# Where the last sweep's bounds, sums and weighted results are made in a one-core graph and expert layer

## The reference

```
x1   = x + segment_sum((ln(x) @ Wg)[src] * w[:, None], dst) + b_g
xf   = ln(x1)
top_w, top_i = top_k(xf @ Wgate + bgate, 2);  top_w = softmax(top_w)
out  = x1 + sum over the two chosen experts e of
           top_w[e] * (gelu(xf @ W1[e] + b1[e]) @ W2[e] + b2[e])
```

## Time and profile before

| what | value |
|---|---|
| median of 3 runs | 900.51 us (893.99, 900.51, 902.76) |
| the profiled execution | 891.33 us, its span 889.6 us |
| mean granted clock of TensorE | 0.942 of full speed |
| PE busy | 716.7 us, 81% |
| DVE busy | 486.4 us, 55% |
| ACT busy | 347.0 us, 39% |
| POOL busy | 605.5 us, 68% |
| q0 (GpSimd's indirect transfers) | 69.14 MB |
| q1 (SyncE's transfers) | 67.56 MB |
| q10 (ScalarE's transfers) | 50.97 MB |

### The profile page before, as it was taken

The page is one execution under the profiler, slowest core; times in us unless marked ns, Lnnn a source line. Parts: engine busy times, 40 slices in busy tenths (PEclk is TensorE's granted clock), DMA queues, the critical chain, the costliest instruction groups (busy, mean ns, idle before and its releaser), DMA issues. The chain is left out here.

```text
span 889.6 us, 15451 instructions
## 1 busy us (share of the span) xinstructions
PE 716.7 (81%) x5265; PEld 703.1 (79%) x5265; DVE 486.4 (55%) x1333; ACT 347.0 (39%) x629; POOL 605.5 (68%) x607
## 2 busy tenths in 40 slices
PE   1067669787199998988899999999999876898891
PEld 0067668686199998978899999989998876898890
DVE  5514212344235477584247867844556877667760
ACT  4312000101024455344244653635546552567770
POOL 6377777777677777777777787777788737023553
PEclk9999999997589999798899999999999999899996
DMA  7897864796468888793888799677767964647742
GB/s 202 260 356 214 226 198 116 203 276 188 123 189 254 246 248 255 203 284 109 230 246 291 227 278 306 192 200 233 254 206 199 269 195 124 210 125 226 201 81 40
DMA packets 121216, 188.68 MB, mean 212 GB/s; under 512 B 20636, under 2 KB 93467, under 8 KB 121008
## 3 DMA queue, kind: packets, MB, share of 16 engines
q0 software_dynamic: 34464, 69.14, 28.2%
q1 hardware_dynamic: 54796, 67.56, 25.8%
q10 hardware_dynamic: 31876, 50.97, 18.3%
HBM read 134.54 MB, written 52.98 MB: 211 GB/s over the span
## 5 line engine op out<-in xcount | busy, mean ns | idle before, releaser
L667 POOL DMA_INDIRECT G<-xn_d,src_t x416 | 427.9, 1029 | 143.5 <-issue 116.4
L916 PE MATMUL ps_agg<-S,G 128*128 128x48 f32 x1664 | 252.4, 317 | 55.6 <-DMA G<-xn_d,src_t 54.9
L916 PEld LDWEIGHTS ps_agg<-S,G 128*128 128x128 f32 x1664 | 249.8, 237 | 59.4 <-issue 51.7
L836 ACT ACTIVATE hf<-ps_h,b_t 128x256 f32<-128x256 f32 x264 | 110.4, 469 | 241.7 <-PE ps_h L1044 230.1
L1044 PE MATMUL ps_h<-y_hi,w_hi 128*128 128x256 f32 x528 | 153.6, 291 | 18.6 <-DVE w_lo L1272 8.0
L1044 PE MATMUL ps_h<-y_hi,w_lo 128*128 128x256 f32 x528 | 150.1, 284 | 0.0
L1044 PE MATMUL ps_h<-y_lo,w_hi 128*128 128x256 f32 x528 | 149.5, 283 | 0.0
L1491 DVE TENSOR_TENSOR h_lo<-hf,h_hi 128x512 fp32r<-128x512 f32 x132 | 90.6, 693 | 91.9 <-ACT h_hi L839 87.0
L1240 DVE TENSOR_TENSOR S<-iota_w,rel_t 128x192 f32<-128x192 f32 x104 | 36.9, 360 | 179.2 <-PE ps_agg L916 173.3
L1272 DVE TENSOR_TENSOR w_lo<-w_raw,w_hi 128x1024 fp32r<-128x1024 f32 x104 | 124.7, 1222 | 7.0 <-ACT w_hi L794 7.0
L794 ACT ACTIVATE w_hi<-w_raw 128x1024 fp32r<-128x1024 f32 x104 | 102.0, 1047 | 56.5 <-PE ps_agg L916 49.8
(11 more groups left out here) (197 smaller groups left out, 612.3 us busy)
## 6 DMA issues: line engine op xcount, KB each, us to landing
w_raw<-in_L_ffn_W ACTq DMA_DIRECT2D x48, 1024.0 KB, 6.2
y_d<-fill SPq DMA_DIRECT2D x30, 388.5 KB, 5.8
yg<-y_d SPq DMA_DIRECT2D x35, 259.0 KB
y_d<-fill SPq DMA_DIRECT2D x32, 259.0 KB
G<-xn_d,src_t POOLq DMA_INDIRECT x416, 2.9
y_d<-fill SPq DMA_DIRECT2D x48, 129.5 KB, 3.0
w_raw<-in_L_ffn_W SPq DMA_DIRECT2D x4, 1024.0 KB, 9.3
r_d<-ost SPq DMA_DIRECT2D x12, 256.0 KB, 6.8
```

The source lines that it names most:

```text
L667: pool.indirect_dma_start(G[:, k, :], None, xn_d, bass.IndirectOffsetOnAxis(src_t[:, n, c:c + 1], 0)).then_inc(main.gathered[n % NR], 16)
L836: nc.scalar.activation(hf[:, j % 2, m, :], ps_h[:, j % 2, m * T:(m + 1) * T], ACT.Gelu, bias=b1_t[:, e * KH + c:e * KH + c + 1]).then_inc( ...
L916: return nc.tensor.matmul(ps_agg[:, k // GT % 2, m * WIN:(m + 1) * WIN], G[:, k, m * 128:(m + 1) * 128], S[:, k, :], start=start, stop=stop)
```

## The change

The bounds part of `sweep_tables` becomes `sweep_bounds` and runs on VectorE in v = 22, behind the second low step of the weights of v = 23. The rest becomes `sweep_rows` and stays where it was. SyncE loads only set 0's sums in v = 21; those of sets 1 and 2 follow in v = 22, behind a wait for ScalarE's first high step of W2 of v = 23. The order of the combine steps within a set becomes two blocks at a time, both experts of each. The 8 steps right before the last sweep and the 7 behind its second expert are gone from there: all 22 that remain come behind its first expert. The sums of set 1 are stored behind the first expert, together with those of set 2. In the loop of the last sweep `results_to_add` moves from behind `tile_low` to between the third and the fourth `hidden_low`.

```diff
     COMBINE_AT = {AHEAD - 1: 6, AHEAD: 12}
+    assert sum(COMBINE_AT.values()) >= 2 * FIRST + 2 * 2 * -(-(RINGT * TH // 2 - FIRST) // 2)
...
                 if HEAD_U[v] == NP and HEAD_U[v - 1] < NP:
                     sp.wait_ge(main.used, RING + NG * GT)
                     load_sums(SETS[0])
+                if v == AHEAD - 1:
+                    sp.wait_ge(s_hi2, STEPS * LOADS[AHEAD] + 1)
                     load_sums(SETS[1])
                     sp.wait_ge(ch.lin, NB)
                     load_sums(SETS[2])
...
             store_sums(SETS[0])
-            store_sums(SETS[1])
             for i, e in enumerate(SWEEP[STILL]):
...
-                if i == 1:
+                if i == 0:
+                    store_sums(SETS[1])
                     store_sums(SETS[2])
...
-            def sweep_tables():
+            def sweep_bounds():
...
                 dve.sem_inc(q.route, 1)
+
+            def sweep_rows():
+
                 own(V.tensor_tensor(shift[:, :], room_tile[:, :], first_f[:, :], ALU.subtract))
...
             def combine(s):
 
-                for j in range(2):
-                    for b in range(s.a, s.z):
+                pairs = [range(b, min(b + 2, s.z)) for b in range(s.a, s.z, 2)]
+                for pair in pairs:
+                    for j, b in ((j, b) for j in range(2) for b in pair):
                         if j == 0 and b == s.a:
                             dve.wait_ge(s_sums[s.index], 32 * len(s.chunks))
                             dve.wait_ge(s_kept[s.index], 32 * (s.z - s.a))
                         if j:
-                            dve.wait_ge(s_combined[s.index], b - s.a + 1)
+                            dve.wait_ge(s_combined[s.index], 2 * (pair[0] - s.a) + b - pair[0] + 1)
...
                 if v == AHEAD:
-                    sweep_tables()
+                    sweep_rows()
...
                 for j in range(NQ - 2):
                     beside()
                     low_step()
+                    if v == AHEAD - 1 and j == 0:
+                        sweep_bounds()
                 if v == AHEAD - 1:
                     combine_some(COMBINE_AT[v])
...
-            combine_some(combined_upto(SETS[1]) - sum(COMBINE_AT.values()))
-            for s in SETS[:2]:
-                dve.wait_ge(s_combined[s.index], 2 * (s.z - s.a))
+            dve.wait_ge(s_combined[0], 2 * FIRST)
+            dve.wait_ge(s_combined[1], 2 * (RINGT * TH // 2 - FIRST))
...
                     for j in range(1, NQ):
                         hidden_low(g, j)
+                        if j == 2:
+                            results_to_add(r - 1)
                     tile_low(g + 1, r + 1)
-                    results_to_add(r - 1)
...
-                if i < 2:
-                    combine_some(BLOCKS - SECOND)
+                if i == 0:
+                    combine_some(2 * BLOCKS - sum(COMBINE_AT.values()))
             results_in(end - 1)
             results_to_add(end - 1)
```

More of the change, by code:

```diff
@@ L1540, in combine_some @@
                     next(combined)
-            def combined_upto(s):
-                return sum(2 * (t.z - t.a) for t in SETS[:s.index + 1])
             tile_low(0)
```

## The result

The changed kernel takes 886.62 us (median of 20 runs, 882.01 to 889.27) against 897.03 us (20 runs, 887.49 to 902.76) for the kernel before, timed in turn with it. The ratio is 0.990, 95% interval 0.988 to 0.9919: 10.4 us faster. Forecast were 884.5 us and a gain of 16.0. The time is inside the range, yet the forecast came that close only because it started from a median of 900.51 that more runs put at 897.03.

The account below looks back on a forecast made before the run. The prediction took GpSimd's late-started adds, with TensorE's chain beneath, to bound the kernel. It summed 8.0 + 4.8 + 3.2 = 16.0 us, from 900.51 to 884.5 us, range 876 to 896 us.

Parts of the forecast that it names:

- Loads of sums: Loading sets 1 and 2 later ends ScalarE's wait for W2 of v = 23; everything behind moves 2.6 us earlier.
- The wait costs nothing unless the 1.66 MB are still in flight: SyncE's new wait for W2's first high step does not delay tile 22's store, unless sums still transfer; through at 727.
- Start of the last sweep: No hole for bounds before tile 24; VectorE's first bounds read takes 1.4 us; tile 24's result starts 11.5 us earlier.
- TensorE without a hole before tile 24: Sign that the forecast holds: TensorE does not stand idle before it starts tile 24.
- 22 steps behind the first expert: VectorE's combine steps, set 2's after its gathers land, let tile 25's result start 9.0 us earlier, 8.0 after lost clock.
- the front: All up to the start of tile 25's result: 8.0 us gained after 1.0 taken off for lost clock.
- the sign of a failed forecast: A TensorE hole at tile 25 of 8 us or more means the 22 steps are in the wrong place.
- Weighing amid a tile: Weighing before the fourth `hidden_low` starts the next weights' low steps 0.8 us earlier at six expert starts: 4.8 us.
- GpSimd's end: GpSimd starts near 768 instead of 789 and catches up; last copy 16.0 us earlier, 3.2 of it GpSimd's own.
- Sum: 8.0 + 4.8 + 3.2 = 16.0 us gained over the whole kernel, from 900.51 to 884.5 us.
- half of it: Rival, chance 0.23: W2 late by itself, store and gathers behind the sums; 9.8 us gained, 890.7 us.
- Instruction fetch: By the skill's rule VectorE's whole 3.95 us stall at its first bounds would stay, losing 2.2 us of the gain.

Follow-up runs that it names:

- `b_plain`: Kernel before, unedited, profiled again; from VectorE's low part of tile 23's rows to the end 171.2 us (172.5 in its first profile).
- `u_loads`: Changed kernel with the sums of all three sets loaded in v = 21 again; from VectorE's low part of tile 23's rows to the end 163.2 us.
- `a_plain`: Changed kernel, unedited, timed and profiled again; 885.44 us against 894.91 for the kernel before, ratio 0.988.
- `u_set2`: Changed kernel with set 2's combine steps and stores behind the second expert; from VectorE's low part of tile 23's rows to the end 163.0 us.
- `u_weigh`: Changed kernel with the weighing behind the low part of the next rows again; from VectorE's low part of tile 23's rows to the end 171.7 us.
- `b_weigh`: Kernel before with only the weighing moved between third and fourth `hidden_low`; from VectorE's low part of tile 23's rows to the end 169.4 us.
- `w_held`: Changed kernel, weight loads behind the first expert held until set 2's gathers landed; from VectorE's low part of tile 23's rows to the end 161.5 us.
- `store_held`: Changed kernel, stores of sets 1 and 2 held until set 2's steps are done; VectorE's low part of tile 23's rows to end 164.9 us.
- `u_bounds`: Changed kernel with the bounds made in v = 23 again; from VectorE's low part of tile 23's rows to the end 162.4 us.
- `sums_late`: Changed kernel with set 2's sums issued behind the load of tile 24; from VectorE's low part of tile 23's rows to the end 162.0 us.

## Why the forecast was right, and where its sum was not

- **Loads of sums.** W2's wait went, and the store of tile 22 is issued 2.5 us earlier (13.15 to 10.62), forecast 2.6. "The wait costs nothing unless the 1.66 MB are still in flight": they were. From 725 to 735 the transfers ran at 235 GB/s, and the first gather came at 14.8, forecast 13.7. By `b_plain` the hole itself varies from launch to launch (2.79 to 6.66), and against that profile, with its store at 9.3, the changed kernel's store is 1.3 us later. By `u_loads` the late loads give the end next to nothing.
- **Start of the last sweep.** No hole for the bounds, as forecast. Tile 24's rows were late instead, 5.52 us, for their load sits behind the same store; the prediction had named "TensorE without a hole before tile 24" as a sign, and it failed. VectorE's first read of its bounds took 1.68 us, forecast 1.4. The sum came out nearly right here: tile 24's result was forecast at 30.1 after t0 and began at 30.7, behind the rows at 30.3.
- **22 steps behind the first expert: the step that was mis-sized.** Forecast for tile 25's result was 45.9 after t0; it is 52.4. The 6.5 us are: first gather 1.1; issue of the 14 gathers 0.5 (21.1 for 20.6); **landing of the last 3.0 (7.24 for 4.2)**; and 1.9 between the last step and the end of `ost` (3.4 for 1.5: two idle stretches of 1 us that the count of busy times left out). The clock took 1.5 us (7.29 for 5.76) where I had 1.0. So the front gave 54.9 - 52.4 - 1.5 = 1.0 us instead of 8.0. With the second profile of either kernel the difference ahead of the clock is -0.4 to 4.1 us: that the front gave anything is not shown, that it did not give 9 is. The landing price was misread: 4.2 is the median of the 14 in the earlier trace rows, and the one that counts is the last, which took 6.6 us (the same row's maximum). That is 2.4 of the 3.0; the rest is within what launches differ by (6.3 in `a_plain`). What I wrote as the sign of a failed forecast, a hole of 8 us or more, was there (8.09), though not in the second profile (4.43). The conclusion I tied to it, that the steps are in the wrong place, `u_set2` does not bear out: elsewhere they cost GpSimd what they give TensorE.
- **Weighing amid a tile.** Forecast 4.8 us. At the last `ost` the gain is 152.76 - 146.53 = 6.2, of which 1.0 is the front: 5.2. `u_weigh` loses 5.5 by undoing it.
- **GpSimd's end.** Forecast 3.2 us; from the last `ost` to the last copy it was 8.35 us and is 4.49: 3.9 (9.68 and 4.51 in the second profiles: 5.2). `u_weigh` shows that it hangs on the ninth result being weighed early, as the prediction had it.
- **Sum.** 1.0 + 5.2 + 3.9 = 10.1 us, against 10.0 measured and 16.0 forecast. Next to it stands my rival "half of it" with 9.8 us, whose mechanism (store and gathers behind the sums) was at work, at 1.1 us instead of 6, since W2 was not late by itself. That the forecast ended 2.1 us from the time is owed to the base: 5.6 us too much gain from a start 3.5 us too high. That closeness is luck.
- **Instruction fetch.** VectorE stood 1.68 us at its first bounds in the changed kernel (1.69 in `a_plain`), 3.95 and 3.92 in the two profiles of the kernel before and 2.63 in `b_weigh`, where SyncE issues the stores of sets 0 and 1 just ahead of and during that wait; in the changed kernel the first of them is issued as it ends. The Trainium skill (Runtime: NRT & Kernel Launch, Instruction fetch mechanics) would keep the whole stall, the branch being the same. The measurements do not bear it out beyond 1.7 us. No run moved the stores alone, so that they are the rest is argued and not shown.

Open: why the work ahead of t0 is 200 us longer on some chips, and how far SyncE's stores of the nodes are what lengthens the last landings; no run moved those of set 0 (`result<-G`, `result<-xr`).

## What to carry to other kernels

When the end is set by an engine that is far behind, an edit to the others shows little until that engine starts earlier (2 to 3 us here), and then far more (9 to 11): price such edits together, and measure each on top of the other. Of a series of transfers the last one's landing counts, not the median's; and a load moved "later" in a queue must be asked what small, urgent store it now sits ahead of. Compare profiles from the last common event, not from the span's start.

## What the runs showed of the hardware

- Within one series of 14 indirect gathers of the same form the landing was 3.8 us at its shortest and 6.6 at the last (kernel before); in nine other profiles the last one took 5.8 (`w_held`) to 9.05 us (`u_weigh`, `store_held`).
- A store issued behind 1.66 MB of loads on the same queue was usable 4.2 us after its issue (3.9 in `a_plain`), and 7.2 us when issued 3.5 us earlier (`u_bounds`): there the queue, not the issue, set its time. Before, and with only 0.77 MB ahead of it (`sums_late`), it took 3.1.
- After a hole of 8.09 us TensorE's granted clock was 0.70 over the next 5 us, between its levels of 1.2 and 2.4 GHz on the mean, and 1.00 over the 10 us behind them; 48 matmuls took 7.29 us instead of 5.76.
- One unchanged kernel had medians of 897 and 895 us in two of the launch groups and of 1086 to 1102 us in the three others, on other chips.
